# A recurrent mixer and a gated MLP on one core: first tile by plain block products, weight sums moved into it, last tile stored by SyncE

## The reference

```
h   = layernorm(x);  h_prev = h shifted by one token
k, v, r = (h, h_prev mixed per channel) @ W_k, W_v, W_r          # 256 x 256
wkv = exponentially weighted recurrence over the tokens (running max p, numerator q)
x1  = x + (sigmoid(r) * wkv) @ W_o
g   = layernorm(x1)
h   = silu((g @ W1) * s1) * ((g @ W2) * s2)                      # 256 -> 1024
h   = gelu((h @ H1) * sh1);  h = gelu((h @ H2) * sh2)            # 1024 -> 1024, twice
out = x1 + (h @ W3) * s3                                         # 1024 -> 256
```

## Time and profile before

| | |
|---|---|
| median of 3 runs | 1526.47 us (1526.46 to 1527.2) |
| the profiled execution | 1526.88 us |
| its span, first to last instruction | 1525.2 us |
| TensorE busy | 97% of the span |
| first matmul of the first `gate` | 81.92 us |
| first matmul of the second tile's `gate` | 174.63 us |
| last VectorE operation ends | 1517.49 us |
| mean granted clock of TensorE | 0.986 |

### The profile page before, as it was taken

The page is one execution under the profiler, slowest core; times in us unless marked ns, Lnnn a source line. Parts: engine busy times, 40 slices in busy tenths (PEclk is TensorE's granted clock), DMA queues, the critical chain, the costliest instruction groups (busy, mean ns, idle before and its releaser), DMA issues.

```text
span 1525.2 us, 28750 instructions
## 1 busy us (share of the span) xinstructions
PE 1484.8 (97%) x10226; PEld 1324.8 (87%) x10226; DVE 1232.8 (81%) x1595; ACT 1093.4 (72%) x1617; POOL 255.8 (17%) x515
## 2 busy tenths in 40 slices
PE   8499999999999999999999999999999999999997
PEld 5269989898898989989898998989899898998997
DVE  7878787987878888787888878789787878878663
ACT  5858777686867768686776877768686776868664
POOL 0211203112030211204021120301213031120300
PEclk9789999999999999999999999999999999999999
DMA  8957567374665737467474746747565573746663
GB/s 364 370 181 232 142 192 228 110 241 129 203 177 165 244 99 244 117 205 204 141 232 110 237 134 204 216 118 233 136 206 165 178 236 98 249 121 205 179 197 107
DMA packets 95893, 287.78 MB, mean 189 GB/s; under 512 B 9216, under 2 KB 33920, under 8 KB 94848
## 3 DMA queue, kind: packets, MB, share of 16 engines
q1 hardware_dynamic: 87168, 279.11, 56.2%
q0 software_dynamic: 8704, 8.39, 4.7%
HBM read 262.30 MB, written 31.46 MB: 193 GB/s over the span
## 4 chain that ended last, share of the span: by engine, by line
PE 93%; issue 0%; DVE 0%; ACT 0%; POOLq 0%; POOL 0%; DVEq 0%
PE acc L540 28%; PE acc L542 27%; PE att L466 10%; PE acc L514 7%; PE acc L515 7%; PE acc L571 4%; PE acc L573 4%; PE att L476 3%; PE att L445 2%; PE att L515 1%; PE att L514 1%; ACT blocks L786 0%; DVE parts L1236 0%; POOLq L161 0%; DVE op_lo L1193 0%
## 5 line engine op out<-in xcount | busy, mean ns | idle before, releaser
L540 PE MATMUL acc<-op_hi,ring 128*128 128x256 f32 x3584 | 865.2, 286 | 1.4 <-DVE parts L1236 1.4
L542 PE MATMUL acc<-op_lo,ring 128*128 128x256 f32 x3584 | 841.6, 279 | 0.0
L540 PEld LDWEIGHTS acc<-op_hi,ring 128*128 128x128 f32 x3584 | 674.3, 188 | 21.0 <-issue 19.9
L542 PEld LDWEIGHTS acc<-op_lo,ring 128*128 128x128 f32 x3584 | 674.3, 188 | 11.9 <-issue 10.8
L1193 DVE TENSOR_TENSOR op_lo<-blocks,op_hi 128x1024 fp32r<-128x1024 f32 (+1 forms) x272 | 345.9, 1287 | 90.7 <-ACT op_hi L746 88.7
L746 ACT ACTIVATE op_hi<-blocks 128x1024 fp32r<-128x1024 f32 (+1 forms) x272 | 297.4, 1105 | 84.7 <-DVE blocks L1188 81.6
L1538 POOL TENSOR_TENSOR v_sb<-mix_v,v_sb 128x1024 f32<-128x1024 f32 (+1 forms) x17 | 39.0, 2295 | 862.8 <-DVE r_sb L1145 862.8
L514 PE MATMUL acc<-x_hi,w_rnd 128*128 128x512 f32 x448 | 180.3, 402 | 3.0 <-issue 3.0
L515 PE MATMUL acc<-x_lo,w_rnd 128*128 128x512 f32 x448 | 178.4, 398 | 0.0
L786 ACT ACTIVATE blocks<-parts,vec 128x256 f32<-128x256 f32 x256 | 109.2, 497 | 60.9 <-DVE parts L1231 52.6
L786 ACT ACTIVATE blocks<-acc,vec 128x256 f32<-128x256 f32 x256 | 100.3, 475 | 66.8 <-PE acc L542 66.8
(11 more groups left out here) (135 smaller groups left out, 1918.4 us busy)
## 6 DMA issues: line engine op xcount, KB each, us to landing
ring<-scratch SPq DMA_DIRECT2D x448, 512.0 KB, 4.2
x_in<-in_x SPq DMA_DIRECT2D x32, 256.0 KB, 4.5
stage<-in_w_ffn SPq DMA_DIRECT2D x4, 2048.0 KB, 22.5
scratch<-stage SPq DMA_DIRECT2D x8, 1024.0 KB, 19.5
out<-x_next SPq DMA_DIRECT2D x32, 256.0 KB, 4.8
out<-mix_v POOLq DMA_DIRECT2D x32, 256.0 KB, 4.4
scratch<-in_w_ffn SPq DMA_DIRECT2D x6, 1024.0 KB, 32.2
w_raw<-in_w_ffn SPq DMA_DIRECT2D x3, 1024.0 KB, 12.6
```

What stands on the lines that cost most here:

```text
L540: pe.matmul(out, act(w), act(op_hi[:, k, c, :]), start=(begins and c == 0 and m % 2 == 0), stop=False, skip_group_check=True)
L542: mm = pe.matmul(out, act(w), act(op_lo[:, k, c, :]), start=False, stop=(c == QC - 1), skip_group_check=True)
```

## The change

The first tile of the MLP takes the eight plain block products of each layer, in TensorE's `plain`: a block of weights is multiplied with both sequences' halves, so a call of it is 64 matmuls, and there are eight calls. It needs no weight sums. So the eight sums (`block_sum`) and the eight checks of them (`check_sum`) move from the prologue into the first tile, which is written out by itself on every engine (`first_tile`), and a second flag is made at its end and read by TensorE behind it. In the prologue remain eleven checks. The scratch has an eighth block (A21). The sums of both layers are formed in the same place (`AREA`, which overlays operands that the plain tile doesn't use); the second layer's blocks are loaded there again when the first layer's sums are stored and checked.

W1, W2 and W3 are copied from DRAM to DRAM (`w_plain`) and loaded from there straight to `w_rnd`, of which `w_raw` is now another view; the three copies behind the flag are gone. SyncE's order is new throughout: the first layer's blocks A21 and A22 stand between `vec`, `wm` and `s3`. It doesn't wait for the flag before it fills the ring. ScalarE issues an `Exp` before anything else, and its order in the prologue is new. VectorE makes the second layer norm's deviations for each sequence by itself.

In the last tile VectorE adds x1 (`finish_last`), and SyncE stores the result; `keep_x1` and `add_out` of that tile are gone.

The diff, cut to its core and moved to the left:

```diff
+PLAIN_WEIGHTS = (A11, A12, A21, A22)
+PLAIN_OPERANDS = ((B11, T1), (B21, B22))
+PLAIN_BANKS = [((acc0, acc1), (acc2, acc0)), ((acc1, acc2), (acc0, acc2))]
...
-scratch = nc.dram_tensor("scratch", [2, STEPS, 2, P, HALF], F32, kind="Internal").ap()
+scratch = nc.dram_tensor("scratch", [2, STEPS + 1, 2, P, HALF], F32, kind="Internal").ap()
+w_plain = nc.dram_tensor("w_plain", [3, P, W12], F32, kind="Internal").ap()
...
-def rounded(copy, a, n):
...
+AREA = [part_of(stage2, 4 * HALF), part_of(stage2, 6 * HALF), part_of(stage1, 4 * HALF), part_of(stage1, 11 * HALF)]
+STAGED = [part_of(stage1, 0), part_of(stage1, 2 * HALF), part_of(stage1, 7 * HALF), part_of(stage1, 9 * HALF)]
+S3_, S1_, S2_, S4_ = AREA
...
+def refill_plain(steps):
+    for n in steps:
+        sp.wait_ge(pe_half.sem, pe_half.at(0, n + 1))
+        if n + SLOTS < PLAIN_STEPS:
+            load_plain(n + SLOTS)
+        else:
+            slot = ld_ring[n % SLOTS]
+            sp.sem_inc(slot.sem, (USES - (n // SLOTS + 1)) * 16)
+            load_ring(n % SLOTS)
...
+def store_sums(l):
+    for k, (step, src) in enumerate(((S1, S1_), (S3, S3_), (S2, S2_), (S4, S4_))):
+        sp.wait_ge(sums[l], k + 1)
+        to_scratch(l, step, src, st_sums[l])
...
+load_area(A21_)
 sp.dma_start(wm[:], w_mix).then_inc(ld_const, 16)
+load_area(A22_)
 sp.dma_start(s3_row[:], s3.broadcast_to([P, D])).then_inc(ld_const, 16)
-sp.dma_start(w_raw[:, W1_AT:W1_AT + W12], w_ffn[:, 0:W12]).then_inc(ld_w1, 16)
-sp.dma_start(w_raw[:, W2_AT:W2_AT + W12], w_ffn[:, W12:2 * W12]).then_inc(ld_w2, 16)
-for l in range(2):
-    for half in range(2):
-        a = 2 * W12 + l * HH + half * 2 * Q
...
+load_area(A11_)
+load_area(A12_)
+for n, a in enumerate((0, W12)):
+    sp.dma_start(w_plain[n], w_ffn[:, a:a + W12]).then_inc(st_w, 16)
+for k in range(4):
+    sp.dma_start(STAGED[k], raw_block(1, k)).then_inc(ld_raw2, 16)
+sp.dma_start(w_plain[2], w_ffn[:, 2 * W12 + 2 * HH:]).then_inc(st_w, 16)
+sp.wait_ge(st_w, 16 * 3)
...
+sp.wait_ge(st_blocks[0], 16 * 4)
+for n in range(SLOTS):
+    load_plain(n)
+for k, step in ((A11_, A11), (A12_, A12), (A21_, A21), (A22_, A22)):
+    to_scratch(1, step, raw_block(1, k), st_blocks[1])
 keep_x1(0)
-load_x(1)
-sp.wait_ge(st_blocks, 16 * 6)
-for l in range(2):
-    sp.wait_ge(st_sums[l], 16 * 4)
-sp.wait_ge(flag_set, 1)
-for n in range(SLOTS):
-    load_ring(n)
-with sp.Fori(0, NT - 2) as i:
+store_sums(0)
+refill_plain(range(1))
+sp.wait_ge(st_blocks[1], 16 * 4)
+refill_plain(range(1, 4))
+sp.wait_ge(st_sums[0], 16 * 4)
+sp.wait_ge(low_done, RAW_CHECKS + 4)
+for k in range(4):
+    sp.dma_start(AREA[k], raw_block(1, k)).then_inc(ld_raw2, 16)
+refill_plain(range(4, 8))
+store_sums(1)
+refill_plain(range(8, PLAIN_STEPS))
+sp.wait_ge(st_sums[1], 16 * 4)
+load_x(2)
+keep_x1(1)
+stored(0)
+with sp.Fori(1, NT - 2) as i:
     refill(i)
     load_x(i + 2)
     keep_x1(i + 1)
     stored(i)
 refill(NT - 2)
-keep_x1(NT - 1)
 stored(NT - 2)
 refill(NT - 1, last=True)
-stored(NT - 1)
+for k, j in enumerate((1, 0)):
+    sp.wait_ge(dve_last, 2 * k + 2)
+    sp.dma_start(out_tiles[j, NT - 1], out_tok[:, HALVES * j:HALVES * (j + 1), :]).then_inc(st_last, 16)
...
+    def plain(l, block, seqs=range(2)):
+        for s in seqs:
+            k, bank = PLAIN_OPERANDS[block % 2][s], PLAIN_BANKS[l][block // 2][s]
+            if block % 2 == 0:
+                begin_plain(l, block // 2, s)
+            for h in range(2):
+                n = 8 * l + 2 * block + h
+                slot = ld_ring[n % SLOTS]
+                pe.wait_ge(slot.sem, slot.at(0, n // SLOTS + 1))
...
+                        w = ring[:, n % SLOTS, c % 2, m * P:(m + 1) * P]
+                        out = bank[:, m * SEG:(m + 1) * SEG]
+                        pe.matmul(out, act(w), act(op_hi[:, k, c, :]), start=(block % 2 == 0 and c == 0 and m % 2 == 0), stop=False,
+                                  skip_group_check=True)
+                        mm = pe.matmul(out, act(w), act(op_lo[:, k, c, :]), start=False, stop=(block % 2 == 1 and c == QC - 1),
+                                       skip_group_check=True)
+                if s == 1:
+                    pe_half.add(mm)
+    def begin_plain(l, row, s):
+        if l == 0 and row == 0:
...
+    def first_tile():
+        gate(0, range(HC - 1))
+        pe.wait_ge(dve_prod.sem, dve_prod.at(0, 3))
+        transpose_x(WHOLE, 1)
+        gate(0, [HC - 1])
+        plain(0, 0)
+        project(WHOLE, 1, [0, 1, 2])
+        plain(0, 1)
+        project(WHOLE, 1, [3])
+        plain(0, 2)
+        project(WHOLE, 1, [4])
+        plain(0, 3)
+        project(WHOLE, 1, [5])
+        plain(1, 0)
+        plain(1, 1)
+        plain(1, 2)
+        project_out(WHOLE, 1)
+        pe.wait_ge(act_g11.sem, act_g11.at(0))
+        pe.wait_ge(low_done, RAW_CHECKS + SUM_CHECKS)
+        pe.matmul(BANK[2][0:1, 0:SUM_CHECKS], ones[:], low_sums[:, RAW_CHECKS:], start=True, stop=True).then_inc(flag_sum, 1)
+        plain(1, 3)
+        pe.wait_ge(flag_max, 2)
+        last(0, lambda: transpose_x2(WHOLE, 1), True)
+        pe.sem_inc(pe_half.sem, HALF_STEPS - PLAIN_STEPS)
+    if first:
+        first_tile()
+        return
...
 hand_over(pe, [s.of_pe for s in FIRST], WHOLE.of_pe)
 pe.wait_ge(flag_set, 1)
 keep_warm(WARM[6], w_k, BANK[0])
-for l in range(2):
-    pe.wait_ge(st_sums[l], 16 * 4)
 flag = pe.value_load(general[0:1, 0:1], min_val=0, max_val=1)
-with pe.If(flag > 0):
-    mlp(exact=False)
+with pe.If(flag == 0):
+    mlp(exact=True, first=True)
+    pe.wait_ge(flag_set, 2)
+    flag_sums = pe.value_load(general[0:1, 1:2], min_val=0, max_val=1)
+    with pe.If(flag_sums == 0):
+        mlp(exact=True, first=False)
+    with pe.Else():
+        mlp(exact=False, first=False)
 with pe.Else():
-    mlp(exact=True)
+    mlp(exact=False, first=True)
...
-def act_copy_(dst, src):
-    return act.activation(dst, src, ACT.Copy)
+def gelu_plain(l, row, s):
...
+    ready = ((act_g11, act_g12), (act_g21, act_g22))[row][s]
+    done = (((act_hiB11, act_hiT1), (act_hiB21, act_hiB22)), ((act_hiG11, act_hiG12), (act_hiG21, act_hiG22)))[l][row][s]
+    act.wait_ge(ready.sem, ready.at(0, (l + 1) * QC))
+    act.wait_ge(pe_half.sem, pe_half.at(0, 8 * l + (6, 8)[row]))
+    hi(PLAIN_OPERANDS[row][s], ALL, done)
...
     copy_kvr(s, 0, range(DC))
-check_piece(w_raw[:, W2_AT:W2_AT + W12], (ld_w2, 16))
-for n, s in enumerate(FIRST):
-    copy_kvr(s, 0, range(DC, 3 * DC))
+check_raw(0, A22_)
+copy_kvr(FIRST[0], 0, range(DC, 3 * DC))
+for k in range(4):
+    exp(FIRST[0], 0, k)
+exp_r(FIRST[0], 0)
+copy_kvr(FIRST[1], 0, range(DC, 3 * DC))
+check_raw(0, A11_)
...
-    for k in range(4):
-        exp(s, 0, k)
-    exp_r(s, 0)
-check_blocks(0)
-check_sums(0)
-check_blocks(1)
-check_piece(w_raw[:, W3_AT:W3_AT + W3], (ld_w3, 16))
-check_sums(1)
-assert checked[0] == N_CHECKS
-for n, s in enumerate(FIRST):
-    copy_x1(s, 0)
-for n, s in enumerate(FIRST):
-    ln2(s, 0)
-act.wait_ge(flag_set, 1)
-flag = act.value_load(general[0:1, 0:1], min_val=0, max_val=1)
-with act.If(flag == 0):
-    rounded(act_copy_, W2_AT, W12).then_inc(rounded_w2, 1)
+check_raw(0, A12_)
+for k in range(3):
+    check_raw(1, k)
+copy_x1(FIRST[0], 0)
+check_raw(1, 3)
+check_weight(W1_AT)
+copy_x1(FIRST[1], 0)
+check_weight(W2_AT)
+ln2(FIRST[0], 0)
+check_weight(W3_AT)
...
+def first_tile():
+    silu(0, 0)
+    silu(0, 1)
+    silu(0, 2)
+    silu(0, 3)
+    hi01(0, 0, True)
+    silu(0, 4)
+    ln1(WHOLE, 1)
+    silu(0, 5)
+    hi01(0, 1, True)
+    silu(0, 6)
+    copy_x(WHOLE, 1)
+    silu(0, 7)
+    hi23(0, 0)
+    hi23(0, 1)
+    copy_kvr(WHOLE, 1, [0, 1])
+    check_sum(0, 0)
+    copy_kvr(WHOLE, 1, [2])
+    check_sum(0, 1)
+    check_sum(0, 2)
+    check_sum(0, 3)
+    gelu_plain(0, 0, 0)
+    gelu_plain(0, 0, 1)
+    copy_kvr(WHOLE, 1, [3])
+    exp(WHOLE, 1, 0)
+    exp(WHOLE, 1, 1)
+    exp(WHOLE, 1, 2)
+    hi_plain(0, 0, 0)
+    hi_plain(0, 0, 1)
+    copy_kvr(WHOLE, 1, [4])
+    gelu_plain(0, 1, 0)
+    hi_plain(0, 1, 0)
+    gelu_plain(0, 1, 1)
+    hi_plain(0, 1, 1)
+    copy_kvr(WHOLE, 1, [5])
+    exp(WHOLE, 1, 3)
+    exp_r(WHOLE, 1)
+    check_sum(1, 0)
+    check_sum(1, 1)
+    check_sum(1, 2)
+    seed_x(WHOLE, 1)
+    check_sum(1, 3)
+    assert checked[0] == RAW_CHECKS + SUM_CHECKS
+    gelu_plain(1, 0, 1)
+    gelu_plain(1, 0, 0)
+    hi_plain(1, 0, 1)
+    hi_plain(1, 0, 0)
+    copy_x1(WHOLE, 1)
+    gelu_plain(1, 1, 1)
+    hi_plain(1, 1, 1)
+    gelu_plain(1, 1, 0)
+    hi_plain(1, 1, 0)
+    ln2(WHOLE, 1)
+    round_x2(WHOLE, 1)
+    for t in (act_hi45, act_hi6, act_p1, act_p5, act_u2, act_hiT23, act_hiT4):
+        act.sem_inc(t.sem, t.per)
+first_tile()
...
-def combine(l, k, dst, a, b, op, loaded):
-    dve.wait_ge(loaded, 16)
+def combine(l, k, dst, a, b, op):
     if k:
...
-def block_sums(l):
...
+def block_sum(l, k):
+    if l == 0:
+        for block in ((A21_, A22_), (A11_,), (), (A12_,))[k]:
+            dve.wait_ge(ld_raw1[block], 16)
+        dve.wait_ge(low_done, RAW_CHECKS)
+    else:
```

(81 more changed lines are left out.)

222 lines of the change are left out of this document (104 added, 118 removed).

## The result

The changed kernel takes 1516.47 us (median of 4 executions, 1516.07 to 1517.01). The kernel before, run beside it, takes 1526.84 (1526.46 to 1527.62). The ratio is 0.9932, interval 0.9914 to 0.9949: 10.4 us faster, where the sum had 4.9 and the number given, 1522.0, had 4.5. The profiled execution took 1516.69, with a span of 1515.0 us (before 1525.2) and a mean granted clock of 0.995.

A forecast was written before the change was run, and what follows sets the result against it. TensorE was taken as the bound, behind a prologue bound by VectorE and ScalarE in turn. Terms -13.7 + 7.5 + 0.9 + 1.6 + 1.0 - 2.2 = -4.9 us gave 1521.6, stated as 1522.0; range 1518 to 1527.5.

The forecast's parts named there:

- the read of each flag: At both flags, TensorE's wait, read and arm were taken as 1.0 us each, from VectorE's 1.06 us.
- Front and VectorE: Prologue: mixing starts at 17.0, 3.65 us late; without the sums VectorE's last multiplication comes at 48.8, no longer the bound.
- ScalarE: Prologue: weights land at 50.7, ScalarE reaches them at 50.8 without slack, checks end at 58.7 instead of 68.2.
- Flag to gate: Prologue end: half-clock warm-ups, transposes and flag read put the gate at 68.2 in place of 81.9, -13.7 us.
- Rival 3: Prologue: the clock stays up, so warm-ups and gate run at 2.4 GHz; 1518 to 1519 us; chance 0.10.
- First tile: TensorE's first tile: 64 more matmuls, +7.5 us, and waits of 0.9 and 1.6 us.
- ScalarE's two waits: First tile: TensorE waits 0.9 us for layer 2's first gelu and 1.6 us for the layer norm at the end.
- The second flag: After the first tile's last matmul: wait, read, arm and loop entry, +1.0 us, upper bound 3.0.
- The reloaded area: First tile: layer 2's blocks land at about 51 us; 3 us of slack before VectorE, 6 before TensorE.
- rival 2: First tile: the reloaded area comes late and stops TensorE; slower, over 1529.5 us; chance 0.09.
- Rival 1: TensorE idles 3 us at both flags; third part, clock down behind the second (+2.3); 1528.0 us; chance 0.28.
- Tail: Behind the last matmul: one more VectorE operation, SyncE's store landing after 2.8 us, 1.6 us to the end; -2.2 us.

The follow-up runs named there:

- Experiment 5: The changed kernel with `wm` and `s3` loaded ahead of blocks A21 and A22; 1515.91 us, ratio 0.9926 to the kernel before.
- experiment 9: The changed kernel without the three warm-up multiplications between the first flag's matmul and the first gate; 1514.4 us, ratio 0.9917 to the kernel before.
- experiment 1: The kernel before with TensorE's two arms exchanged, so the exact path is the first arm; 1524.0 us, ratio 0.9979.
- experiment 3: The changed kernel with the first flag's arms exchanged on TensorE, exact path in the second arm again; 1522.18 us, ratio 0.9969 to the kernel before.
- experiment 4: The changed kernel with the exact path in the first flag's second arm, the first arm holding one semaphore instruction; 1516.08 us, ratio 0.9927 to the kernel before.
- experiment 10: The changed kernel with VectorE's sixth gate product moved ahead of `lo01(0, 1)`; 1514.52 us, ratio 0.9918 to the kernel before.
- Experiment 8: The changed kernel with the second flag's arms exchanged on TensorE, exact path in the second arm; 1519.96 us, ratio 0.9949 to the kernel before.
- experiment 2: The kernel before with only the change's tail (VectorE adds x1, SyncE stores the last tile); 1522.8 us, ratio 0.9973.
- experiment 11: The changed kernel with W1 to W3 copied and loaded ahead of layer 2's blocks, `wm` and `s3` first, checks in landing order; 1510.38 us, ratio 0.9893 to the kernel before.

## Why the prediction was right in direction and wrong in size

The change was said to be worth -4.9 us and gave -10.2 in the span. The difference of 5.3 us lies in the prologue (3.5), the first tile (1.2), the middle (0.1) and the tail (0.5). The term that failed is the clock: the prediction priced the last warm-up, the transposes and the gate's first matmuls at the half clock of the kernel before, and they ran at full clock for the most part, 1.5 us less in the prologue and 2.3 us less in the first tile. The second is the read of each flag, put at 1.0 us twice and seen at 0.1 or less.

**Front and VectorE: right.** The mixing was forecast at 17.0, for a DMA, and came at 16.14; VectorE's last multiplication at 48.8, and it came at 47.81. Experiment 5 showed that the delay is real and hidden, which the prediction had not seen: it charged ScalarE some of the late start, where the wait for the weights stands behind it and takes all of it.

**ScalarE: near in its number, with the slack wrong.** The weights were to land at 50.7, and the check of W1 starts at 50.44, when they do. But ScalarE was to come to them at 50.8 and came at 50.44 - 1.21 = 49.23. The copy before stood at 46.73, forecast 48.1, and a check with other work behind it costs 1.9 us (50.44 to the copy at 52.35), while the 2.09 is the distance of two checks in a row. So it stood still for 1.21 us, where less than 1 was to show, and the loads bounded the prologue, as experiment 5 bears out. The last check was to end at 58.7 and ended at 57.7; that is the other 1.0 us of the prologue's 3.5. From 36.88 on the kernel before has fifteen checks, not fourteen; the price used the fourteen distances and is not touched by it.

**Flag to gate: this is the step of the prologue that failed.** It had 9.5 us from the last check to the gate, and 7.0 were measured. 1.5 of the missing 2.5 are the clock: the last warm-up took 1.10 where "2.05" was carried over from the kernel before, and the transposes 1.47 where "2.0" was. 0.9 is the flag: "I take 1.0" was VectorE's row. VectorE's 1.04 us stands in the changed kernel too, but TensorE shows 0.07 between the warm-up's end, 64.67, and the gate. It has a warm-up multiplication of 1.10 us to run while the flag is read. That this covers the read is argued; no run shows TensorE's read bare, since in experiment 9 the wait for `x_lo` took the warm-up's place. Experiments 1, 3 and 4 show the other half of the step right: the far arm cost the 3.03 us. The first two warm-up multiplications were priced rightly, twice as long as at full clock: four matmuls took 3.78 us, where they take 1.99 in the earlier trace rows.

**The clock.** Rival 3, which had only 0.10, named the place of the error but not its path: it had the clock stay up. It did not. TensorE had stood idle for 5.57 us before the flag's sum, and the warm-ups behind it began at the 1.2 GHz level. The clock rose at 62.0 to 62.5 us, in the transposes, with TensorE at work without a break since 57.84. In the kernel before it was up at that point and fell at 76.5 to 77.0, behind breaks of 1.98 and 0.33 us and in one of 0.56. The prediction's argument against rival 3 counted breaks of 2, 0.6 and 3 us. But the 3 us came behind the last warm-up, which already ran at the lower level, so only the shorter ones counted, and of these the change removed the 2 and the 0.33. That much was to be had from the rows before. That the warm-ups bring the clock up is shown by experiment 9, where it is down in the gate without them. That the removed breaks are why it was up here and down before is argued, not shown, for no run put them back alone. The gate at full clock is worth 2.3 us more, which falls into the next stretch.

**First tile.** The 64 extra matmuls are there, 0.117 us apart, +7.5. ScalarE's two waits were forecast at 0.9 and 1.6 and are 0.7 and 1.1, at the places named. The second flag was to cost 1.0 and costs 0.06; eight transposes and sixteen matmuls stand before it, in the time in which it would be read. That they cover the read is argued. Missed was the 1.3 us wait in the gate, which experiment 10 puts down to the order of VectorE's `lo01(0, 1)` and sixth product. With the clock: 7.5 - 2.3 + 0.7 + 1.1 + 1.3 + 0.2 + 0.1 = 8.6 of the measured 9.8; the other 1.2 us stand in no row of the view of waits. By the distances between TensorE's starts, 0.4 of them is one more change from a matmul of a ring block to a projection (0.52 us to the next start in place of 0.12, at four places where the kernel before has three); the rest lies in pieces of 0.1 to 0.3 us, most of them beside the waits, and stays open.

**The reloaded area** came in time for TensorE and not for VectorE: VectorE's eight sums have one wait of 0.7 us for its load, where the prediction gave 3 us of slack, and TensorE has none behind it, so rival 2 did not happen. The prediction had said that VectorE waiting for `stage` would make it wrong; it did wait, for less than the slack behind it.

**Rival 1** did not happen either, but its parts are real. Experiment 8 shows that 3 us at the second flag were one exchange of arms away. Its third part, the clock falling behind that gap, did not come even then.

**Tail.** -2.2 was forecast and -2.7 came. Two errors partly cancel: the store lands after 3.8 us, not 2.8, and only some 0.4 us lie between landing and the end, where 1.6 were carried over from GpSimd's store.

**What the parts are worth.** The exchange of the arms alone gave the kernel before 2.7 us (experiment 1), and undoing it costs the changed kernel 5.6 (experiment 3); the tail is worth 2.7 to 4 (experiment 2). Of the 10.4 us that leaves some 1 to 5 for the plain first tile, the moved sums and the new orders together. They trade 9.8 us more in the first tile for a prologue shorter by 17.2, and some of the 17.2 is the exchange of the arms. No run has the moved sums alone.

## What to carry to other kernels

Before an engine's time at a flag is costed, look at which arm is far behind the branch in the text, and at what that engine still has queued while the flag is read: here a far arm cost TensorE 3 to 4 us, and the read of the flag nothing that shows behind its queued matmuls, though no run shows that read bare. Whether the clock is down behind a gap can't be told from the gap alone; the length of the last matmuls before it shows where the clock stood when it began. And where a load is the next bound, moving an earlier one gained nothing (experiment 5), and moving both, with ScalarE's checks in the new order, gained 6 us (experiment 11).

## What the hardware showed that was not expected

- An idle time of 2.99 us on TensorE, right behind a stretch of dense matmuls at the granted clock of 1.00, left the clock at the 2.4 GHz level (experiment 8). One of 4.07 us, behind 6.4 us of transposes and warm-ups with a break of 0.59, ended at the 1.2 GHz level (experiment 3).
- A far jump of TensorE cost 2.99 and 3.03 us over one copy of the other path (experiment 8 and the kernel before) and 4.07 over two (experiment 3), a near one 0.22.
- A store of 256 KB from SyncE at the end of the kernel landed after 2.2 us in experiment 2 and after 3.3 to 4.3 in the changed kernel and its variants, whose tails are written alike.
